# Output projection of three 32-head attentions: token tile pairs by seven block products in place of eight, sums on GpSimd

## The reference, cut to what matters

```
scores    = q @ k.T * scale (+ bias or mask)        per head, 64 x 64 or 64 x 128
attended  = softmax(scores) @ v                     1024 tokens x (32 heads * 128)
x         = x + attended @ Wo                       Wo: (32 * 128) x 512
```

## Time and profile before

| | |
|---|---|
| median of 3 runs | 4101.07 us (4098.96 to 4109.01) |
| the profiled execution | 4102.87 us, span 4101.0 us, mean granted TensorE clock 0.971 |
| PE busy | 3834.4 us (93%) |
| DVE busy | 2409.6 us (59%) |
| ACT busy | 1405.1 us (34%) |
| POOL busy | 550.7 us (13%) |
| output products (PE busy) | l1x 229.2, l3a 229.5, l3x 117.8 + 115.2 us |
| where the stages lie, us from the span's start | l1x 1337 to 1893, l3a 2690 to 3286, l3x 3335 to 4048 |

### The profile page before, as it was taken

One profiled execution on the slowest core, in us unless ns is written; L12 is line 12 of the kernel. 1 busy time (PEld: TensorE's weight loads), 2 busy tenths in 40 slices (PEclk: granted clock), 3 DMA queues, 4 the chain that ended last, 5 costly groups with the idle time before them and its releaser, 6 DMA issues. The chain is left out here.

```text
span 4101.0 us, 49676 instructions
## 1 busy us (share of the span) xinstructions
PE 3834.4 (93%) x18570; PEld 2048.5 (50%) x18570; DVE 2409.6 (59%) x4054; ACT 1405.1 (34%) x2522; POOL 550.7 (13%) x520
## 2 busy tenths in 40 slices
PE   8899979998989899999999889789999989999998
PEld 3343435554455455554447664345455545555564
DVE  0988955552247444444447658876766665555563
ACT  2988935552233211111113334211111133333331
POOL 1111111220001211100000111121211111000000
PEclk9999999999989999999999989999999999999998
DMA  5111111001100432311001022100001021111110
GB/s 190 54 36 52 55 68 34 31 29 63 41 34 14 181 113 103 119 61 75 0 21 49 1 104 59 66 6 36 21 21 42 1 69 37 37 37 36 42 37 24
DMA packets 133959, 215.31 MB, mean 53 GB/s; under 512 B 42576, under 2 KB 95056, under 8 KB 123104
## 3 DMA queue, kind: packets, MB, share of 16 engines
q1 hardware_dynamic: 133728, 212.19, 14.8%
HBM read 168.12 MB, written 44.04 MB: 52 GB/s over the span
## 5 line engine op out<-in xcount | busy, mean ns | idle before, releaser
L1187 PE MATMUL l3a_po<-l3a_wo,l3a_cT 128*128 128x512 f32 x512 | 229.5, 596 | 1.2 <-ACT l3a_cT L1384 1.2
L555 PE MATMUL l1x_po<-l1x_wo,l1x_cT 128*128 128x512 f32 x512 | 229.2, 592 | 1.2 <-issue 1.2
L1187 PEld LDWEIGHTS l3a_po<-l3a_wo,l3a_cT 128*128 128x128 f32 x512 | 95.6, 190 | 119.9 <-issue 115.5
L555 PEld LDWEIGHTS l1x_po<-l1x_wo,l1x_cT 128*128 128x128 f32 x512 | 95.9, 190 | 115.7 <-issue 115.6
L1075 PE MATMUL l3a_pj<-kvT,l3a_ws 128*128 128x512 f32 x256 | 121.4, 608 | 11.4 <-POOL l3a_ws L979 10.3
L718 DVE TENSOR_TENSOR x<-x,l1x_po 128x512 f32<-128x512 f32 x64 | 44.1, 688 | 143.8 <-PE l1x_po L555 143.8
L1075 PE MATMUL l3x_pj<-kvT,l3x_ws 128*128 128x512 f32 x256 | 122.0, 609 | 2.4 <-DVE l3x_qT L1514 2.2
L1187 PE MATMUL l3x_po<-l3x_wo,l3x_cT 128*128 128x512 f32 x256 | 117.8, 604 | 0.7 <-ACT l3x_cT L1384 0.7
L1187 PE MATMUL l3x_pc<-l3x_wo,l3x_cT 128*128 128x512 f32 x256 | 115.2, 592 | 0.0
L2216 DVE TENSOR_SCALAR_CACHE_REDUCE l0a_keep<-l0a_keep,l0a_scalars 128x1376 uint16<-128x1376 uint16 x64 | 105.4, 1646 | 3.6 <-DVE l0a_scalars L2222 1.5
L2663 POOL TENSOR_TENSOR l0x_q<-l0x_q,l0x_qi 128x512 f32<-128x512 f32 x64 | 65.4, 1042 | 303.7 <-DVE l0x_qi L2951 303.7
(11 more groups left out here) (572 smaller groups left out, 8450.6 us busy)
## 6 DMA issues: line engine op xcount, KB each, us to landing
l1x_kb<-l1x_keys SPq DMA_DIRECT2D x32, 512.0 KB, 4.6
l1x_vb<-l1x_values SPq DMA_DIRECT2D x32, 512.0 KB, 3.3
l1x_keys<-l0a_kv SPq DMA_DIRECT2D x40, 256.0 KB, 2.0
fill_wk<-in_L_xattn_Wk SPq DMA_DIRECT2D x8, 1024.0 KB, 5.9
kvT<-in_L_xattn_Wv SPq DMA_DIRECT2D x8, 1024.0 KB, 5.6
l1x_values<-l0a_kv SPq DMA_DIRECT2D x32, 256.0 KB, 2.3
l1x_wq<-in_L_xattn_Wq SPq DMA_DIRECT2D x8, 1024.0 KB, 6.8
l1x_sbias<-in_L_xattn_bias SPq DMA_DIRECT2D x8, 1024.0 KB, 7.3
```

What stands on the lines that cost most here:

```text
L555: mm = pe.matmul(po[:, t % 2, :], cT[:, u, h, t * P:(t + 1) * P], wo[:, u, h, :], start=h == 0, stop=h == GH - 1)
L1187: mm = pe.matmul(outs[t % 2][:, :], cT[:, h, t * P:(t + 1) * P], wo[:, u, h, :], start=h == 0, stop=h == GH - 1)
```

## The change

Two token tiles (rows 1 and 2 of blocks) by two halves of the head dimension (2 x 2 heads) make a 2 x 2 block matrix, and `wo` another (head halves by column halves of 256). The product of the two is formed by seven block products in place of eight, each of two matmuls on 256 columns. The block sums are formed in SBUF on GpSimd: `mix_cols` (four operations of 128 x 512, once a group, in part in place in `wo`) and `mix_rows` (four of 128 x 256 for each tile pair, in part in place in `cT`). `out` of two tiles becomes `out_low` (products a, and two into bank `po[:, 1]`, announced as p) and `out_high` (b, two more into that bank as q, and c). Products a, b and c of a pair use the same 256 columns of the first bank one after the other; in the last group every second pair uses `pj` for them. VectorE adds them in five parts: a (256 columns), p (512), b (256), q (512), c (the same 256 columns to both halves). In the last group the moments for the next norm stand between these adds. The programs' orders around them change as the diff shows. The kernel's scratch size for dynamic DMA is set to 1024.

```diff
@@ stage_bias (l1x)
+def out_at(n, tt, phase):
+    return 20 * n + 5 * tt + "apbqc".index(phase)
+def rows_at(n, tt, i):
+    return 16 * n + 4 * tt + (3, 1, 2, 4).index(i)
+def cols_at(n, i):
+    return 4 * n + (3, 1, 2, 4).index(i)
+def attended_rows(u, k, tile):
+    return cT[:, u, 2 * k:2 * k + 2, tile * P:(tile + 1) * P]
+def out_block(u, k, half):
+    return wo[:, u, 2 * k:2 * k + 2, half * 256:(half + 1) * 256]
+def first_bank(n, tt):
+    return pj[:, 0, 0:256] if n == GROUPS - 1 and tt % 2 else po[:, 0, 0:256]
...
+        def mix_cols(n):
+            u = n % 2
+            low, high = out_block(u, 0, 1), out_block(u, 1, 1)
+            pool.wait_ge(wo_loaded[u], 8 * (n + 2 - u))
+            if n >= 2:
+                pool.wait_ge(o_ready, out_at(n - 2, 3, "c") + 2)
+            nc.gpsimd.tensor_tensor(wos[:, u, 0], high, low, ALU.subtract).then_inc(cols_mixed, 1)
+            pool.wait_ge(cols_mixed, cols_at(n, 3) + 2)
+            nc.gpsimd.tensor_tensor(low, low, out_block(u, 0, 0), ALU.subtract).then_inc(cols_mixed, 1)
+            pool.wait_ge(cols_mixed, cols_at(n, 1) + 2)
+            nc.gpsimd.tensor_tensor(wos[:, u, 1], high, low, ALU.subtract).then_inc(cols_mixed, 1)
+            pool.wait_ge(cols_mixed, cols_at(n, 2) + 2)
+            nc.gpsimd.tensor_tensor(wos[:, u, 2], out_block(u, 1, 0), wos[:, u, 1], ALU.subtract).then_inc(cols_mixed, 1)
+        def mix_rows(n, tt):
+            u, v = n % 2, tt % 2
+            one, two = (attended_rows(u, k, 2 * tt) for k in range(2))
+            one2, two2 = (attended_rows(u, k, 2 * tt + 1) for k in range(2))
+            if tt == 0:
+                pool.wait_ge(a_copied, 2 * GH * (n + 1) + 1)
+            if tt >= 2:
+                pool.wait_ge(o_ready, out_at(n, tt - 2, "c") + 2)
+            elif n:
+                pool.wait_ge(o_ready, out_at(n - 1, tt + 2, "c") + 2)
+            nc.gpsimd.tensor_tensor(cs[:, v, 0], one, one2, ALU.subtract).then_inc(rows_mixed, 1)
+            pool.wait_ge(rows_mixed, rows_at(n, tt, 3) + 2)
+            nc.gpsimd.tensor_tensor(one2, one2, two2, ALU.add).then_inc(rows_mixed, 1)
+            pool.wait_ge(rows_mixed, rows_at(n, tt, 1) + 2)
+            nc.gpsimd.tensor_tensor(cs[:, v, 1], one2, one, ALU.subtract).then_inc(rows_mixed, 1)
+            pool.wait_ge(rows_mixed, rows_at(n, tt, 2) + 2)
+            nc.gpsimd.tensor_tensor(cs[:, v, 2], two, cs[:, v, 1], ALU.subtract).then_inc(rows_mixed, 1)
         front.roots(pool)
         mix(0)
         pool.wait_ge(mask_ready, 2)
         mask_bias(0, 0)
         for n in range(GROUPS):
             mix(2 * n + 1)
+            if n:
+                mix_rows(n - 1, 0)
+                mix_rows(n - 1, 1)
             if n + 1 < GROUPS:
                 mask_bias(n + 1, 1 - n % 2)
+            if n:
+                mix_rows(n - 1, 2)
+            if n + 1 < GROUPS:
                 mix(2 * n + 2)
+            if n:
+                mix_rows(n - 1, 3)
+            mix_cols(n)
+        for tt in range(T // 2):
+            mix_rows(GROUPS - 1, tt)
...
-        def out(n, u, t):
-            if t == 0:
+        def product(bank, rows, cols, opens):
+            for c in range(2):
+                mm = pe.matmul(bank, rows[:, c], cols[:, c], start=opens and c == 0, stop=c == 1, skip_group_check=not opens)
+            return mm
+        def out_low(n, u, tt):
+            one, two2 = attended_rows(u, 0, 2 * tt), attended_rows(u, 1, 2 * tt + 1)
+            if tt == 0:
                 pe.wait_ge(wo_loaded[u], 8 * (n + 2 - u))
                 pe.wait_ge(a_copied, 2 * GH * (n + 1) + 1)
-            pe.wait_ge(added, T * n + max(t, 1))
-            for h in range(GH):
-                mm = pe.matmul(po[:, t % 2, :], cT[:, u, h, t * P:(t + 1) * P], wo[:, u, h, :], start=h == 0, stop=h == GH - 1)
-            mm.then_inc(o_ready, 1)
+            if n == GROUPS - 1 and tt:
+                if tt >= 2:
+                    pe.wait_ge(added, out_at(n, tt - 2, "c") + 2)
+            elif n or tt:
+                pe.wait_ge(added, out_at(n, tt, "a") + 1)
+            product(first_bank(n, tt), one, out_block(u, 0, 0), True).then_inc(o_ready, 1)
+            if tt:
+                pe.wait_ge(added, out_at(n, tt - 1, "q") + 2)
+            pe.wait_ge(cols_mixed, cols_at(n, 4) + 2)
+            product(po[:, 1, 0:256], two2, wos[:, u, 2], True)
+            pe.wait_ge(rows_mixed, rows_at(n, tt, 1) + 2)
+            product(po[:, 1, 256:512], attended_rows(u, 0, 2 * tt + 1), out_block(u, 0, 1), True).then_inc(o_ready, 1)
+        def out_high(n, u, tt):
+            v, two = tt % 2, attended_rows(u, 1, 2 * tt)
+            pe.wait_ge(rows_mixed, rows_at(n, tt, 2) + 2)
+            pe.wait_ge(added, out_at(n, tt, "a") + 2)
+            product(first_bank(n, tt), cs[:, v, 1], wos[:, u, 1], False).then_inc(o_ready, 1)
+            pe.wait_ge(rows_mixed, rows_at(n, tt, 4) + 2)
+            pe.wait_ge(added, out_at(n, tt, "p") + 2)
+            product(po[:, 1, 256:512], cs[:, v, 2], out_block(u, 1, 1), False)
+            product(po[:, 1, 0:256], two, out_block(u, 1, 0), True).then_inc(o_ready, 1)
+            pe.wait_ge(added, out_at(n, tt, "b") + 2)
+            product(first_bank(n, tt), cs[:, v, 0], wos[:, u, 0], False).then_inc(o_ready, 1)
         def group(n, u, behind):
...
                 if behind:
-                    out(n - 1, 1 - u, 4 * p)
+                    out_low(n - 1, 1 - u, 2 * p)
                 turns(n, 2 * p)
                 if more:
                     step(i + 1, 3)
                 if behind:
-                    out(n - 1, 1 - u, 4 * p + 1)
+                    out_high(n - 1, 1 - u, 2 * p)
                 attend(n, 2 * p)
                 scores(n, 2 * p + 1)
                 if more:
                     step(i + 1, 4)
                 if behind:
-                    out(n - 1, 1 - u, 4 * p + 2)
+                    out_low(n - 1, 1 - u, 2 * p + 1)
                 if more:
                     step(i + 1, 5)
                 turns(n, 2 * p + 1)
                 if behind:
-                    out(n - 1, 1 - u, 4 * p + 3)
+                    out_high(n - 1, 1 - u, 2 * p + 1)
                 if more:
                     step(i + 1, 6)
                 attend(n, 2 * p + 1)
...
-        def add(n, t):
-            dve.wait_ge(o_ready, T * n + t + 2)
-            nc.vector.tensor_tensor(m.x[:, t, :], m.x[:, t, :], po[:, t % 2, :], ALU.add).then_inc(added, 1)
+        def add(n, tt, phase):
+            t, half = 2 * tt + (phase in "pc"), slice(256 * (phase == "b"), 256 * (phase == "b") + 256)
+            dve.wait_ge(o_ready, out_at(n, tt, phase) + 2)
+            if phase in "ab":
+                dst, src = m.x[:, t, half], first_bank(n, tt)
+            elif phase == "c":
+                dve.wait_ge(added, out_at(n, tt, "p") + 2)
+                dst = m.x[:, t, :].rearrange("p (e d) -> p e d", e=2)
+                src = first_bank(n, tt).unsqueeze(1).to_broadcast([P, 2, 256])
+            else:
+                if phase == "q":
+                    dve.wait_ge(added, out_at(n, tt, "b") + 2)
+                dst, src = m.x[:, t, :], po[:, 1, :]
+            nc.vector.tensor_tensor(dst, dst, src, ALU.add).then_inc(added, 1)
+        def add_low(n, tt):
+            add(n, tt, "a")
+            add(n, tt, "p")
+        def add_high(n, tt):
+            add(n, tt, "b")
+            add(n, tt, "q")
+            add(n, tt, "c")
...
                 if behind:
-                    add(n - 1, 4 * p)
-                    add(n - 1, 4 * p + 1)
+                    add_low(n - 1, 2 * p)
+                    add_high(n - 1, 2 * p)
                 scaled(n, u, 2 * p + 1)
                 shift(2 * p + 1)
                 weighed(n, 2 * p + 1)
                 if behind:
-                    add(n - 1, 4 * p + 2)
+                    add_low(n - 1, 2 * p + 1)
                 if more:
                     summed(i + 1, 4)
                 if behind:
-                    add(n - 1, 4 * p + 3)
+                    add_high(n - 1, 2 * p + 1)
                 if more:
                     summed(i + 1, 6)
         def closing():
-            for t in range(T):
-                add(GROUPS - 1, t)
-                if t < T - 1:
-                    dve.wait_ge(added, T * GROUPS - T + t + 2)
-                    ahead.moments(dve, t)
+            n = GROUPS - 1
+            for tt in range(T // 2):
+                add(n, tt, "a")
+                if tt:
+                    dve.wait_ge(added, out_at(n, tt - 1, "q") + 2)
+                    ahead.moments(dve, 2 * tt - 2)
+                add(n, tt, "p")
+                add(n, tt, "b")
+                if tt:
+                    dve.wait_ge(added, out_at(n, tt - 1, "c") + 2)
+                    ahead.moments(dve, 2 * tt - 1)
+                add(n, tt, "q")
+                add(n, tt, "c")
+            dve.wait_ge(added, out_at(n, T // 2 - 1, "q") + 2)
+            ahead.moments(dve, T - 2)
```

(71 more changed lines are left out.)

160 lines of the change are left out of this document (126 added, 34 removed).

## The result

| | before | after |
|---|---|---|
| median, us | 4101.44 (4098.96 to 4109.01, 4 runs) | 4230.47 (4224.61 to 4232.83, 4 runs) |
| span of the profiled execution | 4101.0 | 4230.5 |
| granted TensorE clock, mean | 0.971 | 0.952 |

The ratio is 1.031, 95% interval 1.0297 to 1.0323: slower by 129 us. Forecast: 4191, range 4112 to 4245.

What follows compares the result with a forecast made beforehand. The prediction took all three stages to be bound by TensorE. It summed l1x -17, l3a +102 (77 + 26 + 24 - 26, and 1.5) and l3x +5 to +90 us, 4191 us as a median, range 4112 to 4245.

Steps and rivals of the forecast that it cites:

- Price of a product: All three stages: 216 ns per half-width instruction, 6.05 us per tile pair against 6.86, saving 26 us per stage.
- Waits in l3a: TensorE waits in l3a for VectorE's adds on one shared bank: 77 us, plus 26 us from GpSimd's sums.
- The walk: Following VectorE's program through an l3a group to each add: 11.2 us of TensorE waits in each of six groups.
- three hits of 1.24 us: In each l3a group, GpSimd's sums delay VectorE ahead of three late adds by 1.24 us each; 26 us over seven groups.
- The second pair: In l3a, the pair's last product waits 4.95 us for the add of b, behind softmax work, a sum and a rotation.
- the first pair: In l3a, out_high waits 3.7 us for the add of a, which stands behind a rotation on VectorE.
- the third and fourth: In l3a, these pairs' waits on the shared bank, with a rotation between two adds, together 2.55 us a group.
- Contention: GpSimd's sums stretch VectorE's two-input operations in l3a, adding 26 us; bounds nothing or twice that.
- Clock: In l3a, 14 waits of 4 us and above each cost 1.7 us at half clock: 24 us, at most 48.
- l3x and l1x: l3x: 15 of waits, 14 from column sums, 2 at end, minus 26: +5 us. l1x: 7 + 1.5 - 26 = -17.
- Waits only: Rival, chance 0.25: l3a's waits stay but no contention or clock loss; +19, 4120 us.
- Everything doubles: Rival, chance 0.10: contention 52 and clock 48 in l3a (+152), l3x +19, l1x -10; 4262 us.

Runs made afterwards that it cites:

- experiment 1: Changed kernel with l3a put back to its old function, l1x and l3x in the new form; 4087.5 us, ratio 0.9965.
- experiment 2: Changed kernel with l1x and l3x put back to their old functions, only l3a in the new form; 4246.9 us, ratio 1.0349.
- experiment 4: Changed kernel with VectorE's late adds in l3a moved ahead of the rotations and softmax sums, nothing added or removed; 4111.5 us, ratio 1.0022.
- experiment 6: Changed kernel with GpSimd's row sums of l3a and column sums of l3x cut to 8 columns from the second group; 4158.7 us, ratio 1.0140.
- experiment 8: Changed kernel with l3a's adds early, a second PSUM bank, two rotations after the last adds, later column sums in l3x and l3a's first group; 4069.0 us.
- experiment 9: The kernel of experiment 8 with l3a's row sums cut to 8 columns from the second group; 4060.1 us, ratio 0.9904.
- experiment 7: Changed kernel with old l3a, and l3x's column sums started only after the next group's keys are scaled; 4065.5 us, ratio 0.9908.
- experiment 5: Changed kernel with twelve unread 128x512 matmul instructions ahead of the two long waits of each l3a group; 4197.9 us, ratio 1.0229.

## Why the prediction was right, and where it was off

**Direction, stage and mechanism: right.** The saving arrived in l1x, and l3a lost several times as much to one shared bank. Experiments 1 and 2 place the loss in l3a, and experiment 4 shows that VectorE's order makes most of it.

**Price of a product: right.** 0.86 us, 216 ns to the next start, in every stage.

**Waits in l3a: right in sum.** A group waited 6.52 + 6.14 + 0.31 + 2.01 + 0.87 = 15.85 us. The walk had 3.7 + 4.95 + 2.55 = 11.2, with three hits of 1.24 us 14.9. The second pair is exact (6.14 against 6.19), the first 1.6 us too low (stretching of 2.55 us), the third and fourth 0.6 too high. Over the stage 107.6 us, forecast as 77 + 26; the groups lie 99.6 us apart, forecast as 91 to 96. That the sum came out is in part luck. With short sums (experiment 6) the waits of the same group are 2.92, 4.93, 0.31, 0.77 and 0.87 us, 9.8 in all: the lateness by itself was put 1.4 us a group too high, at the first and the third pair, and the stretching too low.

**Contention: the right kind, and too small.** Forecast 26 us of waits; experiment 6 took away 35, from six of the seven groups. Ahead of the first pair alone the sums were worth 3.6 us (6.52 to 2.92), where 1.24 was taken. The group of VectorE's two-input operations that grew most in l3a, before and after (busy us, mean ns):

```profile
L1481 DVE TENSOR_TENSOR l3a_part<-l3a_raw,l3a_sinq 64x512 f32<-64x512 f32 x128 | 96.3, 752 | 4.0
```

```profile
L1715 DVE TENSOR_TENSOR l3a_part<-l3a_raw,l3a_sinq 64x512 f32<-64x512 f32 x128 | 122.2, 955 | 4.0
```

25.9 us here and 14.5 on three further lines, 40 in all. In the order of experiment 8, where VectorE is busy for 83% of the stage, 16 us of stretching cost 11 (experiment 9). The Trainium skill ("GPSIMD Engine Reference", Key points) says that GpSimd shares its SBUF interfaces with VectorE, with contention for instructions with two SBUF inputs or in a 2-port mode. The traces agree on two inputs: those of the group above went from 752 to 955 ns on the mean. A one-input TENSOR_SCALAR of the unpacking also went from 0.49 to 1.38 us; no run here shows in which mode it ran. The prediction quoted only the part on two inputs, and took 0.7 us for each of the codes' operations, where these rows of experiment 7 show 0.9.

**Clock: the step that was mis-sized.** "The 14 waits of 4 us and above in l3a would each pay" 1.7 us: 24 us, at most 48. The runs show about 50. The product b of the first pair comes every 99.6 us on the mean of six steps from group to group (2727.03 to 3324.46), 20.5 more than the 79.1 of before. Of these 15.85 are waits, and the products give back 4 x 0.81, so that 7.9 us of slow clock are left in a group, 47 in the six and some more in the last. TensorE's busy time gives it a second way: 663.65 us, against 613.59 for the same work in experiment 8, is 50. Two things were wrong. A stretch at half clock lasted 6.8 us behind most waits, not 3.3 as behind the one wait of the earlier trace rows; the trace of before already had a longer one, 10 us from 2685.8 at the opening of l3a. And there were three in a group, not two: the waits of 2.01 and 0.87 us, with a product between them, brought one as well. I had set the limit at 4 us from no row. The experiment that takes the slow clock away and leaves the lateness (5) moved 34 us, for two of the three.

**End and opening.** l3a's opening waits 12.1 us for a rotation, 8.7 before: the first group's column sums stretch it, and in experiment 8, which places them behind the rotations, it is 8.7 again. That is 3.4 us that the prediction didn't have; 107.6 + 3.4 + 50, less the 20 that the products give in busy time (experiment 8), is 141 of the 142.3 us. This splits the stage's idle and busy time and is no separate check.

**l3x and l1x: right in sum, both terms somewhat smaller.** In l3x idle time rose by 22 us (26.4 to 48.5) and busy time fell by 21.5, against 31 and 26. The column sums were worth 16 to 20 us (experiments 6 and 7), where 14 were taken, well inside the bounds of 0 to 28. In l1x idle rose by 4.5 us, against 8.5, and busy fell by 22.1. The products give 4 us less than 26 in both, and the clock explains most of it. The same new form of l1x takes 529.5 to 535.8 us in nine traces. In the three fastest (experiments 1, 6 and 8) TensorE is busy for 508.0 us, 25.3 less than before; the kernel after has two more stretches of 3.4 us at half clock in that stage than experiment 1. In l3x busy time is 710.1 to 710.4 us in experiments 6, 8 and 9, 26 less than before, and 714.7 in the kernel after. A product behind even a short wait also takes 0.94 us instead of 0.86 (from 3058.24 to 3059.18 in l3a). So that l1x came to -17.6 against -17 is partly luck: both of its terms were about 4 us too large, and the stage itself varies by more.

**Rivals.** "Waits only" (4120 us) falls to the clock. "Everything doubles" had the clock right (48) and the contention too high (52, where experiment 6 takes 35 away), and it also needed l3x at +19, which came to +0.6.

## What to carry to other kernels

Before fewer matmuls are bought with a chain through one PSUM bank, walk through the consumer's program and see where it is when each link is wanted: here a reordering of VectorE alone moved 119 us, and the saved products are worth 26 at most in a stage. Price a wait of TensorE with the slow clock behind it, and several short waits in a row like a long one. And when a second engine takes over sums in SBUF, place them beside work that reads PSUM or beside idle time, and look again after each reordering: moving four operations per group gave l3x 16 us, and a rotation moved beside such sums lost 3.5 us a group in l3a. With l3a left as it was the kernel came to 4065.5 us, 0.9% faster than before.

## What the hardware did that I had not expected

- A single-input TENSOR_SCALAR of 128x512 in f32 (0.49 us) took up to 1.38 us beside a GpSimd sum of 128x512. The two-input operation next to it went from 0.69 to 1.64 us. Beside sums of 128x256 two-input operations mostly took 1.10.
- Two-input operations of VectorE that read one input from PSUM kept their time whatever GpSimd did. All of one kind in l3a after, min/median/max ns, and below it the kind with both inputs in SBUF:

```profile
L1748 DVE TENSOR_TENSOR l3a_raw<-l3a_saves,l3a_pj x48: 672/678/689, 2633.1 to 3354.0; 128x512 f32<-128x512 f32 x48
```

```profile
L1715 DVE TENSOR_TENSOR l3a_part<-l3a_raw,l3a_sinq x128: 684/1098/1752, 2634.6 to 3360.2; 64x512 f32<-64x512 f32 x128
```

So the adds themselves cost what was planned; what stands ahead of them does not.
- In the kernel after the granted clock fell to half behind two waits with one product between them, the first of 1.6 to 2.1 us and the second of 0.87, in all six groups where they come. Behind 2.25 and 0.87 us it did so in five groups of six (experiment 4, in one of them behind the 2.25 alone), behind 2.01 and 0.87 in five of six (experiment 5), and behind 0.77 and 0.87 in none of five (experiment 6).
